# Perceiver layer on one core: the recurrence's output projection as three f32r products instead of one f32 product

## The reference, cut to what matters

```
x = x + xattn(layernorm(x), ctx)                      # 32 x 64 x 512, context 32 x 1601 x 512
# recurrence, over 64 steps, for 32 rows of 512:
z   = sigmoid(layernorm(x) @ Wg.T + bg)
h_t = df * h_(t-1) + (1 - df) * z_t * (x_t - (h_(t-1) @ Wr.T + br))
x   = x + layernorm_w_b(h) @ Wo.T + bo
# experts: softmax router, top 2 of 8
x   = x + sum over 2 experts of w_e * ((silu(x3 @ G_e) * (x3 @ U_e)) @ D_e),   x3 = layernorm(x)
```

## Time and profile before

| | us |
|---|---|
| time, median of 3 runs | 1310.67 (1310.32 to 1310.84) |
| the profiled execution, its own time | 1311.46 |
| its span | 1309.7 |
| TensorE busy in the span | 1212.5 (93%) |
| VectorE busy | 732.6 (56%) |
| first yT of the scan to last yT of the scan | 736.48 to 895.62 |
| start of the experts' first load (SyncE) | 922.49 |

### The profile page before, as it was taken

One profiled execution on the slowest core, in us unless ns is written; L12 is line 12 of the kernel. 1 busy time (PEld: TensorE's weight loads), 2 busy tenths in 40 slices (PEclk: granted clock), 3 DMA queues, 4 the chain that ended last, 5 costly groups with the idle time before them and its releaser, 6 DMA issues. The chain is left out here.

```text
span 1309.7 us, 29558 instructions
## 1 busy us (share of the span) xinstructions
PE 1212.5 (93%) x10417; PEld 730.7 (56%) x10418; DVE 732.6 (56%) x1569; ACT 411.9 (31%) x892; POOL 589.2 (45%) x642
## 2 busy tenths in 40 slices
PE   0799999999999999999989699997699999999993
PEld 0444444444443444444467466664588888888882
DVE  4555666555566655556379668887623323233235
ACT  2334444434445443444146111112211211112110
POOL 1033332223333223333059568887386564530972
PEclk9999999999999999999989799998799999999997
DMA  8646654445665444566065778752123444412556
GB/s 275 234 168 210 218 201 141 171 155 197 216 216 183 149 163 163 207 218 209 10 219 145 222 238 304 262 175 108 41 91 126 152 160 144 160 52 71 156 161 187
DMA packets 99250, 225.22 MB, mean 172 GB/s; under 512 B 14152, under 2 KB 30664, under 8 KB 95088
## 3 DMA queue, kind: packets, MB, share of 16 engines
q1 hardware_dynamic: 83712, 181.86, 40.6%
q0 software_dynamic: 10288, 33.57, 7.5%
q10 hardware_dynamic: 5184, 8.92, 2.1%
HBM read 178.95 MB, written 45.35 MB: 171 GB/s over the span
## 5 line engine op out<-in xcount | busy, mean ns | idle before, releaser
L325 POOL TENSOR_TENSOR wb<-wb,w 128x512 f32<-128x512 f32 x120 | 149.3, 1276 | 337.7 <-ACT wb L508 337.7
L395 PE MATMUL S<-ctxT,x 32*64 32x416 f32 (+1 forms) x4096 | 186.4, 510 | 16.5 <-DVE ctxT L637 15.9
L395 PEld LDWEIGHTS S<-ctxT,x 32*64 32x64 f32 x4096 | 110.7, 133 | 93.5 <-issue 44.4
L619 DVE STREAM_TRANSPOSE ctxT<-ctx_one 128x1024 f32<-128x1024 f32 (+1 forms) x128 | 114.8, 946 | 22.1 <-DMA ctx_one<-in_ctx_dram 21.9
L430 PE MATMUL O<-ctx_one,probsT 128*64 128x512 f32 (+1 forms) x448 | 110.4, 608 | 0.0
L522 ACT ACTIVATE x<-S,w2R,w3R 128x128 f32<-128x128 f32 x256 | 93.4, 490 | 19.2 <-PE S L386 19.2
L1971 POOL TENSOR_TENSOR w_low<-w_low,w_high 128x2048 fp32r<-128x2048 f32 x21 | 96.7, 4607 | 1.7
L2156 DVE TENSOR_TENSOR f_hL<-f_TH,f_hH 128x512 fp32r<-128x512 f32 x39 | 27.0, 692 | 122.0 <-ACT f_hH L2109 122.0
L2114 ACT ACTIVATE sg<-f_G 128x512 f32<-128x512 f32 x39 | 23.3, 597 | 194.7 <-PE f_G L2056 194.7
L508 ACT ACTIVATE wb<-w,hcb 128x512 f32<-128x512 f32 x120 | 77.6, 746 | 0.0
L644 DVE TENSOR_REDUCE mx<-S 128x1 f32<-128x832 f32 x16 | 16.4, 1024 | 102.5 <-PE S L395 102.5
(11 more groups left out here) (287 smaller groups left out, 2484.4 us busy)
## 6 DMA issues: line engine op xcount, KB each, us to landing
ctx_one<-in_ctx_dram SPq DMA_DIRECT2D x64, 512.0 KB, 4.5
x<-in_ctx_dram SPq DMA_DIRECT2D x16, 1536.0 KB, 8.6
ctx_two<-in_ctx_dram SPq DMA_DIRECT2D x16, 1536.0 KB, 9.4
ctx_one<-in_ctx_dram SPq DMA_DIRECT2D x64, 256.0 KB
w_low<-_L_ffn_gate_up_proj_dram POOLq DMA_DIRECT2D x10, 1024.0 KB, 8.3
f_xt<-routed_x SPq DMA_DIRECT2D x39, 256.0 KB, 2.7
routed_y<-f_yt SPq DMA_DIRECT2D x39, 256.0 KB, 2.1
w_low<-_L_ffn_gate_up_proj_dram SPq DMA_DIRECT2D x6, 1024.0 KB, 10.4
```

The lines of the kernel that those rows point to most:

```text
L325: pool.tensor_tensor(wb[:, slot, b], wb[:, slot, b], w0[:, c], ALU.add).then_inc(wb_ready, 1)
L395: last = pe.matmul(S[64 * b:64 * b + 64, a, 0:tiles * Q], qr[a * Q:(a + 1) * Q, k, 64 * b:64 * b + 64], ctxT[a * Q:(a + 1) * Q, 0:tiles, b ...
L619: return dve.transpose(ctxT[:, pos:pos + n, b], src[:, i:i + n, :].rearrange("p t (k r) -> p t k r", r=Q))
```

## The change

The product with Wo in the recurrence is computed as y Wo = yH WoH + yH WoL + yL WoH in f32r. ScalarE makes `yH` of each tile (`take_y`), VectorE makes `yL` (`low_y`) between step 1 and `stats2`, and likewise `WoH` (`take_wo`) and `WoL` (`low_wo`) once. `stats2` stays on VectorE. `turn_y` now comes ahead of the product in step 0, and each step has three f32r products instead of one f32 chunk. The high part of the experts' weights, `w_high`, is allocated from the start, and the recurrence's own tiles lie in it; expert 0's high parts are made on ScalarE in k = 7, 9 and 11. At the end of the recurrence the residual and the statistics of tile 15 move from body 17 to body 16, ahead of `row_places(12)`; the last count is a product of its own in `prefix(15)`, into `Bo`; two constants of the plan are made in body 16. In the experts, the low parts come first on VectorE, and `token_places` and `token_weights` go into body 0.

```
--- before.py
+++ after.py
-        self.Wr, self.Wo = (sb(n, [P, sh.C, sh.D]) for n in ("wr_rows", "wo_rows"))
-        self.ln_w, self.ln_b, self.bo = (sb(n, [P, sh.D]) for n in ("lnw_b", "lnb_b", "bo_b"))
-        self.gate_w = sb("gw", [sh.E, sh.D])
+        self.Wr, self.Wo = ex.room(0, 0), ex.room(0, 1)
+        self.ln_w, self.ln_b, *perm = ex.rows(0, 2)
+        self.bo = sb("bo_b", [P, sh.D])
+        self.gate_w = ex.rows(1, 2)[2][0:sh.E]
...
+    HIGH_AT = [ex.SLOTS + 4 + 2 * part for part in range(ex.PARTS)]
...
-        yT = [sb(f"yT{s}", [P, C, ST, B]) for s in range(2)]
-        WoT = sb("WoT", [P, C, D])
-        xn3 = [sb(f"xn3{s}", [P, D]) for s in range(RING - 2)] + rw.u
-        xn3T = sb("xn3T", [P, C, P])
+        steps = [rows.rearrange("p (t e) -> p t e", t=ST) for rows in ex.rows(2, 1)]
+        ut, ct = steps[0:2], steps[2:4]
+        scan_row, passed, *plan_rows = ex.rows(2, 2)
+        H, m, gd, g = (scan_row[:, i * P:(i + 1) * P] for i in range(4))
+        yT = [rows.rearrange("p (c t b) -> p c t b", c=C, t=ST) for rows in y_rows]
+        WoH, WoL = sb("WoH", [P, C, D], F32R), sb("WoL", [P, C, D], F32R)
+        yH, yL = (sb(n, [P, C, P], F32R) for n in ("yH", "yL"))
+        xn3 = xn3_early + rw.u
...
-                    pe.wait_ge(wo_ready, n - 1)
+                    pe.wait_ge(wo_low, n - 1)
...
-            def wo_chunk(j, s, c):
-                if c == 0:
-                    if has(j - 2):
-                        pe.wait_ge(x2_ready, j - 1)
-                    if first(j):
-                        pe.wait_ge(wo_ready, C)
-                last = pe.matmul(Wb[s][:], yT[s][:, c].rearrange("p t b -> p (t b)"), WoT[:, c, :], start=(c == 0), stop=(c == C - 1))
-                if c == C - 1:
-                    last.then_inc(wo_done, 1)
+            def wo_product(j, s, first_op, n):
+                for i in range(first_op, first_op + n):
+                    low_y, c = i // (2 * C), i % C
+                    if i == 0:
+                        if has(j - 2):
+                            pe.wait_ge(x2_ready, j - 1)
+                        if first(j):
+                            pe.wait_ge(wo_ready, C)
+                            pe.wait_ge(wo_low, C)
+                        pe.wait_ge(yH_ready, j + 1)
+                    if i == 2 * C:
+                        pe.wait_ge(yL_ready, j + 1)
+                    last = pe.matmul(Wb[s][:], (yL if low_y else yH)[:, c, :], (WoL if i // C == 1 else WoH)[:, c, :],
+                                     start=(i == 0), stop=(i == 3 * C - 1))
+                    if i == 3 * C - 1:
+                        last.then_inc(wo_done, 1)
             def turn_y(j, s):
                 if first(j):
-                    pe.wait_ge(wo_ready, C - 1)
+                    pe.wait_ge(wo_low, C - 1)
...
+                if j == TILES - 1:
+                    pe.matmul(Bo[:, 0:P], ones[:], oh[:, None, :].to_broadcast([P, P // E, E]), start=True, stop=False)
+                    pe.matmul(Bo[:, 0:P], ones[:], rt.acc[:, None, :].to_broadcast([P, P // E, E]),
+                              start=False, stop=True).then_inc(cnt_full, 1)
...
-                        for c in ((), (0,), (1,), (2, 3))[st] if k1(k) else (st,):
-                            wo_chunk(k - 1, 1 - s, c)
                         if st == 0:
                             turn_y(k - 1, 1 - s)
+                        first_op, n_ops = ((0, 0), (0, 2), (2, 4), (6, 6))[st] if k1(k) else (3 * st, 3)
+                        wo_product(k - 1, 1 - s, first_op, n_ops)
...
-            pe.wait_ge(places_ready, TILES)
-            pe.matmul(Rk[:, 0:P], ones[:], rt.acc[:, None, :].to_broadcast([P, P // E, E]), start=True, stop=True).then_inc(cnt_full, 1)
...
-                act.copy(WoT[:, :, k * P:(k + 1) * P],
+                act.copy(WoH[:, :, k * P:(k + 1) * P],
                          (Yb, XT)[k % 2][:].rearrange("p (c e) -> p c e", c=C)).then_inc(wo_ready, 1)
+            def take_y(j, s):
+                act.wait_ge(yT_ready, ST * (j + 1))
+                if has(j - 1):
+                    act.wait_ge(wo_done, j)
+                act.copy(yH[:], yT[s].rearrange("p c t b -> p c (t b)")).then_inc(yH_ready, 1)
...
+                if scan:
+                    take_y(k, n % 2)
                 if scan and has(k - 3):
                     exp(k - 3)
...
+                if k in HIGH_AT:
+                    act.wait_ge(ex.w_in[0], 16 * ex.PARTS)
+                    act.wait_ge(wo_ready, C)
+                    ex.first_high(act, HIGH_AT.index(k))
...
+            def low_wo(k):
+                dve.wait_ge(wo_ready, k + 1)
+                part = slice(k * P, (k + 1) * P)
+                dve.tensor_tensor(WoL[:, :, part], (Yb, XT)[k % 2][:].rearrange("p (c e) -> p c e", c=C),
+                                  WoH[:, :, part].bitcast(F32), ALU.subtract).then_inc(wo_low, 1)
+            def low_y(j, s):
+                dve.wait_ge(yH_ready, j + 1)
+                if has(j - 1):
+                    dve.wait_ge(wo_done, j)
+                dve.tensor_tensor(yL[:], yT[s].rearrange("p c t b -> p c (t b)"), yH[:].bitcast(F32), ALU.subtract).then_inc(yL_ready, 1)
...
-                dve.tensor_tensor(rt.acc[:], rt.acc[:], oh[:], ALU.add).then_inc(place_step, 1)
-                dve.wait_ge(place_step, ops + 1)
+                if j < TILES - 1:
+                    dve.tensor_tensor(rt.acc[:], rt.acc[:], oh[:], ALU.add).then_inc(place_step, 1)
+                else:
+                    ops -= 1
+                dve.wait_ge(place_step, ops + (1 if j < TILES - 1 else 2))
...
+                    low_wo(1)
+                if has(k - 2) and k != TILES + 1:
...
+                    low_wo(3)
                 if has(k - 1):
+                    low_y(k - 1, 1 - s)
                     stats2(k - 1)
...
+                    low_wo(2)
+                if has(k - 2) and k != TILES + 1:
                     stats3(k - 2)
...
+                if k == TILES:
+                    residual(k - 1, 1 - s)
+                    stats3(k - 1)
                 if has(k - 4):
                     row_places(k, n, loads)
-            walk(dve, body)
+                if k == TILES:
+                    plan_constants()
...
+            def plan_constants():
+                dve.wait_ge(iotas, 2)
+                then(dve.tensor_copy(tile_no[:], tile_no_i[:]), dve.tensor_copy(step_no[:], step_no_i[:]))
+                then(dve.tensor_scalar(step_no[:], step_no[:], float(P), None, ALU.mult))
+            walk(dve, body)
             dve.wait_ge(plan_consts, 1 + 2 * E)
             dve.wait_ge(cnt_full, 1)
-            then(dve.tensor_copy(tile_no[:], tile_no_i[:]), dve.tensor_copy(step_no[:], step_no_i[:]),
-                 dve.tensor_copy(cnt[:], Rk[:, 0:E]))
-            then(dve.tensor_scalar(step_no[:], step_no[:], float(P), None, ALU.mult))
+            then(dve.tensor_copy(cnt[:], Bo[:, 0:E]))
...
+    def room(self, slot, part):
+        return self.high[:, slot, part].bitcast(F32)
+    def rows(self, slot, part):
+        return [self.high[:, slot, part, c].bitcast(F32) for c in range(self.high.shape[3])]
+    def first_high(self, act, part):
+        act.copy(self.high[:, 0, part], self.low[:, 0, part].bitcast(F32)).then_inc(self.w_high, 1)
...
-            def high_first(e, part):
-                act.copy(high[:, e, part], ex.low[:, e, part].bitcast(F32)).then_inc(w_high, 1)
-            act.wait_ge(ex.w_in[0], 16 * PARTS)
-            high_first(0, GATE)
-            high_first(0, UP)
             take_x(0, 0)
-            high_first(0, DOWN)
...
+                    token_places()
                 gate(t)
+                if not later(t, 1):
+                    token_weights()
...
+            low_first(0, GATE)
+            low_first(0, UP)
+            low_x(0, 0)
+            low_first(0, DOWN)
             stored_counts()
             rank_weights()
-            low_first(0, GATE)
-            low_x(0, 0)
-            low_first(0, UP)
-            low_first(0, DOWN)
-            token_places()
-            token_weights()
```

More of the change, by code:

```diff
@@ L774, in __init__ @@
                             decay[c * P:(c + 1) * P].rearrange("(o d) -> o d", o=1).to_broadcast([sh.B, P])) for c in range(sh.C)]
-        self.WrT = sb("WrT", [P, sh.C, sh.D])
-        self.w_perm = [sb(f"w_perm{i}", [P, sh.C, P]) for i in range(2)]
-        self.w_scaled = sb("w_scaled", [P, sh.D])
+        self.WrT = ex.room(1, 0)
+        self.w_perm = [rows.rearrange("p (q e) -> p q e", q=sh.C) for rows in perm]
+        self.w_scaled = ex.rows(1, 2)[3]
         self.w_sum, self.w_nmean, self.bo_col = (sb(n, [P, sh.C]) for n in ("w_sum", "w_nmean", "bo_col"))
@@ L781, in __init__ @@
         self.loaded = stack.enter_context(nc.semaphore("recurrence_w_in"))
-        self.u, self.c = ([sb(f"g_{n}{s}", [P, sh.D]) for s in range(2)] for n in "uc")
+        rows = ex.rows(1, 1)
+        self.u, self.c = rows[0:2], rows[2:4]
```

(6 more changed lines are left out.)

40 lines of the change are left out of this document (16 added, 24 removed).

## The result

The changed kernel takes 1316.95 us (median of 6 runs, 1315.35 to 1317.73) against 1310.76 us (1310.16 to 1313.24) of the kernel before on the same chip: a ratio of 1.0040, interval 1.0027 to 1.0053. It is slower, by 6.2 us from median to median and by 3.5 to 6.9 us by the interval; the prediction was 1317.6. The profiled execution took 1317.73 us, its span 1315.7 (before 1311.46 and 1309.7).

What follows compares the result with a forecast made beforehand. It took VectorE to bound the scan tile's first two intervals, GpSimd the third, TensorE and VectorE the fourth. Terms -2.2 + 12.35 + 0.7 - 0.3 - 3.6 = +6.95 us gave 1317.6 us, range 1307.5 to 1324.5.

Steps and rivals of the forecast that it cites:

- A: Product with Wo in the scan: shorter f32r chunks on TensorE show only in interval 4, 0.15 us a tile; -2.2 us.
- interval 4: Scan tile, step 3 to the next tile's step 0, 2.57 us: TensorE and VectorE both bind, about 0.3 us apart.
- B: low_y on VectorE between step 1 and stats2, where there is no gap: 0.85 us a tile, +12.35 us in all.
- C: Four WoL subtractions on VectorE in the first tiles: three hidden, the fourth, in k = 1, on the path; +0.7 us.
- D: ScalarE's added work, take_y and the three copies for expert 0: covered by later readers, 0 us.
- E: Memory: the recurrence's tiles lie in w_high, transfers keep their queues and order; 0 us.
- F: End of the recurrence: later last places against a shorter passage from last cast to the count's comparison; -0.3 us.
- G: Start of the experts: TensorE's idle before the second gate product and the clock's fall after it go; -3.6 us.
- 1: Rival: TensorE bounds the scan and VectorE's operation fits under it; -20 us, 1290.6 us, chance 0.05.
- 2: Rival: low_y costs 0.68, partly taken up, and intervals 1 and 4 shrink; -2.7 us, 1308.0 us, chance 0.13.
- 3: Rival: TensorE's clock falls in the scan as its busy share drops; +20 on top, 1338 us, chance 0.04.
- 4: Rival: the experts' restart gap stays, low_x(1) finding something else in front; the sum loses 3.6, 1321.2 us; no chance given.

Runs made afterwards that it cites:

- e2: Changed kernel without low_y, the third group of products reading yH again: 1326.81 us, ratio 1.0104 to the kernel before; the total is worthless since routing changed.
- e3: Changed kernel with low_y done twice in each tile, the first time into a spare tile: 1340.43 us, ratio 1.0211 to the kernel before.
- e7: Changed kernel with low_y done once only, as zero, all twelve products kept: 1306.91 us, ratio 0.9973 to the kernel before.
- e4: Changed kernel with low_y one step later, ahead of stats3, and yL used in step 3 alone: 1310.23 us, ratio 0.9988 to the kernel before.
- e1: Changed kernel with only the product with Wo back to one f32 product: 1310.48 us, ratio 0.9987 to the kernel before.
- e12: Changed kernel with tile 15's residual and statistics one body later, where they stood before the change: 1316.20 us in one execution.
- e8: Changed kernel with VectorE's old order at the start of the experts: 1319.18 us, ratio 1.0052 to the kernel before.
- e6: Changed kernel with the f32 product back and y's statistics on ScalarE without layernorm's epsilon: 1308.84 us, ratio 0.9978 to the kernel before.
- e9: Kernel of e7 with x's load issued on ScalarE's queue instead of SyncE's: 1309.18 us, ratio 0.9993 to the kernel before.
- e5: Changed kernel with y's statistics moved from VectorE to ScalarE, without layernorm's epsilon: 1311.10 us, ratio 1.0000 to the kernel before.

## Why the prediction was right, step by step

The forecast was slower by 6.95 us in the profiled execution, and it was slower by 6.27. The terms, as the intervals of the scan summed over all tiles show them:

- **A, TensorE's saving**, predicted at -2.2 us with -5 as its bound: it is -5.1, the bound, and -4.5 of it lie in interval 4. In the steady tiles that interval shrank by 0.33 us and not by 0.15. The step that failed is that "the cast on VectorE still meets the bias addition". It doesn't. The logits and the prefix product, which VectorE's chain of places waits for, stand behind the shorter chunk on TensorE as well. The first instruction of that chain, before and after, 0.64 and 0.36 us behind the start of the transpose:

```profile
825.48 0.17 DVE L1689 TENSOR_REDUCE r_nmx<-Lg 128x1 f32<-128x8 f32 x1 [0.32 <-PE Lg L1512]
```

```profile
829.47 0.17 DVE L1724 TENSOR_REDUCE r_nmx<-Lg 128x1 f32<-128x8 f32 x1
```

  So the cast, at 830.24, begins before the bias addition of 830.39 does. It took 0.22 us instead of 0.44, and VectorE now waits 0.24 us for `predict`. I had moved one reader of TensorE forward, `predict`, and left the other in place. The tile k = 10 is the check: there the cast starts 0.22 us later against the transpose than elsewhere, for a reason that the profile doesn't name, and so behind the bias addition again:

```profile
851.74 0.73 POOL L1428 TENSOR_TENSOR w_high<-w_high,bo_b 128x256 f32<-128x256 f32 x1
```

```profile
851.81 0.68 DVE L1768 CAST pl_i<-plf 128x2 int32<-128x2 f32 x1 [0.18 <-issue]
```

  It takes 0.68 us, and interval 4 of that tile has 2.58 us, nothing less than before. Not all of the -4.5 is TensorE's saving, though: three of the eleven tiles from k = 4 to 14 weren't near 10.06 us before (k = 5, 6 and 9, with 10.34, 10.20 and 10.44), and in these three interval 4, which had 2.74 to 2.94 us, shrank by 0.50 to 0.70.
- **B, `low_y`**, predicted +12.35 us: +11.8, from 11.13 in the second interval of k = 4 to 15 and 0.70 in k = 2 and 3. It costs 0.96 in the steady tiles, where I took 0.85. I put the operation "behind all of `gd`"; in fact the two start together and `low_y` takes 1.02 us, and it is the next GpSimd operation, `g`, that is drawn out. The Trainium skill (SBUF — State Buffer, who interferes with whom) has the two exclude each other for a whole instruction. The trace agrees that they get in each other's way: the 0.68 us of `low_y` is the one behind the scan, with GpSimd idle, and the median of all sixteen is 1.01. It doesn't agree in size: in k = 2 to 4, where `gd` was 0.2 us ahead as I had assumed, `low_y` took 0.81 us and not my 0.95. So the upper bound of 0.95 came out nearly right by luck, from an overlap that isn't the one in these tiles. e2, e3 and e7 confirm the sign and the place of the term, e4 that it is the place that makes the price.
- **C, `WoL`**, +0.7 with 1.5 as its bound: +1.5, the bound. The second interval of k = 1 has 4.02 us instead of 2.50, and it has the same 4.02 in e2, which has no `low_y`: there VectorE waits 0.83 us for `predict`, which stands on TensorE behind the first products, and these wait for the fourth subtraction. The first three subtractions were hidden.
- **D and E**, 0: `yH` takes 0.62 us and the copies for expert 0 1.9 us each on ScalarE, and no interval with them differs from one without. The scan of e1, which has the copies and the memory but not the product, differs from before by 0.24 us in all.
- **F, the end of the recurrence**, -0.3: it is +0.57 from the last yT to the first gate product. The last places came 0.6 us later, as forecast (18.88 us after the last yT instead of 18.26), and e12 shows that the moved residual gives 0.8 against that. The step that failed is the gain of 1.0 us from the count product and the constants. The plan did get shorter, 5.48 us instead of 6.62 from the last cast into `pl_i` to the last cast of the plan, but the experts didn't start sooner for it: what I hadn't seen is that the plan isn't the path. The path goes from the last places over GpSimd's last scatter, whose landing the program waits for before it leaves the recurrence. VectorE's first instruction of the experts comes 4.99 to 5.01 us after the end of that scatter in all fourteen traces (921.55 - 916.55 before, 930.70 - 925.71 after), whatever VectorE did meanwhile: its own wait is 0.87 us in the kernel before and 2.0 us in the thirteen others, the 1.1 us by which the plan got shorter. That is the +1.09 of the table. No run moved the scatter by itself, so what of the 5 us is the landing (2.7 us from issue, the median) and what the rest isn't split.
- **G, the start of the experts**, -3.6: -2.84. The restart gap and the slow second gate product are gone (-3.67); the low clock in the first gate product lasted 0.83 us longer. That part differs from one execution to the next: over the twelve kernels with the new order the stretch from the first gate product to TH took 10.11 to 11.54 us, a gain of 2.4 to 3.8, and the predicted -3.6 is 10.35. By e8, though, the part that I gave to the clock (-1.67) needn't have been lost with the old order.

Against the forecast A was off by -2.9 us, B by -0.5, C by +0.8, F by +0.9 and G by +0.8, and these nearly cancel. That the total is right to 0.7 us is luck in part; the direction rests on B, which was right. The bounds of the terms, added up, give +1 to +15 us and not the +1 to +13 written there. Of the signs named beforehand, the last yT came 8.5 us later and not 11, and interval 4 shrank by 0.33 in the steady tiles, just short of the 0.35 that was to count as wrong, and by more in three others.

The rivals: **1** fell, as `m` of step 2 starts 2.63 us after the transpose where it had been 1.67. **2** was right that interval 4 gains more than 0.15 (0.33), but interval 1 shrank by 0.02 only, and `low_y` cost 0.96 and not 0.68. **3** didn't come about here, and e3 shows that it can with a tile 0.9 us longer. Its figure of 8.5 us busy in a tile was too low: 10.04 - 1.08 is 8.96, and the trace has 9.45 of 10.67. **4** fell by the rows at 945.

## What to carry to other kernels

Where an engine has a gap-free stretch between two steps of a recurrence, every instruction put there costs its full length times the tiles, whatever the fullest engine saves; before adding one, look for the interval in which that engine waits for another and put it there: the same `low_y` cost 0.95 us in one and 0.50 in the other, the difference between slower and even. The same holds at the end of a stage: a chain cut by 1.1 us gave nothing, since another engine's last transfer was what the next stage waited for. And an engine that hands on sooner moves all its readers: follow each of them before a saving is cut down to one that still waits. A scan that is made faster also asks for its transfers sooner: here the five tiles k = 6 to 10, with weights on the way, didn't go under 50 us in any of the fourteen traces, whichever queue the late load stood on; why isn't shown.

No version beat both kernels clearly. e7's 1306.91 leaves the low part of y out; e6's 1308.84, the f32 product with ScalarE's statistics, is faster than before by 0.22% [0.10, 0.35] and leaves out an epsilon.

## What the runs showed of the hardware that I had not expected

- Where `low_y` and `gd` meet, the operation after them is drawn out as well: `g` took 0.80 us there and 0.46 in the tile's other steps.
- TensorE's granted clock fell in the middle of a loop in e3: it was idle for 1.47 us ahead of a `predict` and for less elsewhere, and within that `predict` or soon behind it the clock went to the low level (1.2 GHz) and stayed there for 3 to 7 us, seven times in the scan. Other tiles of e3 with the same wait kept the high level, and so did e9 with a single wait of 2.39 us and the changed kernel from k = 4 on, with waits up to 0.94 us. So the length of the wait alone doesn't decide it. The Trainium skill (TensorE: Matmul & The Clock Gate, Part 1: The HAM clock gate) has the gate go by how busy the array has been; e3 agrees as far as it shows a fall within a loop that never stops for long.
- The first gate product, most of it at the low clock, took 4.54 to 5.97 us over the thirteen kernels with the same instructions in it, and their first yT comes anywhere from 734.5 to 738.4 us. From a difference of 2 us between two single executions nothing follows.
- ScalarE reads its accumulator in a separate 0.19 us instruction behind each pass: e5's statistics come to 2 x 0.60 + 2 x 0.19 + 0.19 + 0.29 = 2.06 us of instructions, against 0.68 + 0.18 + 0.15 on VectorE.
